# Half of the first attention's row maxima moved from the experts' stage in among its first exponentials, which go one head at a time

## The reference, cut to what matters

```python
# L0: group norm, 8 heads of 32 channels, full softmax attention, residual
weight = softmax(einsum('bct,bcs->bts', q * scale, k * scale))
a = einsum('bts,bcs->bct', weight, v)
x = xf + proj(a)
# L1: layer norm, causal attention over 8 heads, residual
t = t + attn(ln_t(t))
# experts: layer norm, top 2 of 32 experts of width 64, sigmoid gates, all computed, gated
h = relu(einsum('td,edh->teh', xt, keys))
t = t + einsum('teh,te,ehv->tv', h, w, values)
```

## Time and profile before

| | |
|---|---|
| median of 3 runs | 4272.27 us (4267.15 to 4276.54) |
| span of the profiled execution | 4288.4 us |
| PE busy | 3671.0 us (86%) |
| DVE busy | 2027.4 us (47%) |
| ACT busy | 1710.8 us (40%) |
| POOL busy | 771.3 us (18%) |
| DMA | 263.84 MB, mean 62 GB/s |
| maxima on DVE (line 1044) | 983.4 us in 1024 instructions |

### The profile page before, as it was taken

One profiled execution on the slowest core, in us unless ns is written; L12 is line 12 of the kernel. 1 busy time (PEld: TensorE's weight loads), 2 busy tenths in 40 slices (PEclk: granted clock), 3 DMA queues, 4 the chain that ended last, 5 costly groups with the idle time before them and its releaser, 6 DMA issues.

```text
span 4288.4 us, 55007 instructions
## 1 busy us (share of the span) xinstructions
PE 3671.0 (86%) x18386; PEld 2033.9 (47%) x18386; DVE 2027.4 (47%) x2857; ACT 1710.8 (40%) x2732; POOL 771.3 (18%) x1051
## 2 busy tenths in 40 slices
PE   5898789987898878988889888898889987999867
PEld 3344563445634456344653445534464344644445
DVE  6334572355723566245652446424563345733533
ACT  1354335442354423634236342453334533354422
POOL 0000251002600035000430005300052001610035
PEclk7798899988998889989899798997898978999879
DMA  3011340114402143021420224202341113411134
GB/s 89 1 40 30 91 115 24 40 30 107 116 7 55 29 113 102 16 51 41 114 79 16 55 55 110 65 19 51 71 113 46 31 39 80 119 31 40 30 82 117
DMA packets 229749, 263.84 MB, mean 62 GB/s; under 512 B 137424, under 2 KB 139472, under 8 KB 229328
## 3 DMA queue, kind: packets, MB, share of 16 engines
q1 hardware_dynamic: 73808, 124.88, 12.1%
q0 software_dynamic: 155648, 135.17, 11.9%
HBM read 145.80 MB, written 9.44 MB: 36 GB/s over the span
## 4 chain that ended last, share of the span: by engine, by line
PE 57%; DVE 13%; DMA 11%; issue 8%; ACT 6%; POOL 2%; SPq 2%; DVEq 0%; ACTq 0%; POOLq 0%
PE ps_acc L586 9%; PE ps_two L684 9%; PE ps_acc L595 9%; DVE tops L1044 7%; DMA probs<-gates_dram 7%; PE ps_two L653 7%; PE ps_one L530 4%; DMA expert_sb<-experts_dram 3%; PE ps_one L531 3%; PE ps_one L532 3%; PE ps_one L684 3%; POOL nat L488 2%; SPq L414 1%; PE ps_one L718 1%; PE ps_one L725 1%
## 5 line engine op out<-in xcount | busy, mean ns | idle before, releaser
L1044 DVE TENSOR_REDUCE tops<-ps_two 128x1 bf16<-128x1024 f32 (+7 forms) x1024 | 983.4, 988 | 547.6 <-PE ps_two L656 401.1
L653 PE MATMUL ps_two<-stacks 96*128 96x512 f32 (+2 forms) x1792 | 664.5, 469 | 267.6 <-DVE tops L1044 198.6
L852 ACT ACTIVATE probs<-ps_two 128x1024 f32<-128x1024 f32 (+1 forms) x704 | 666.4, 963 | 385.0 <-PE ps_two L684 301.3
L476 POOL DMA_DIRECT2D expert_sb<-experts_dram x256 | 143.2, 561 | 2743.0 <-DVE rsum L1051 2608.9
L653 PEld LDWEIGHTS ps_two<-stacks 96*128 96x128 f32 x1792 | 355.8, 221 | 468.1 <-DVE tops L1044 270.9
L684 PE MATMUL ps_two<-stacks 97*128 97x512 f32 (+3 forms) x1408 | 525.4, 455 | 40.0 <-ACT probs L852 24.1
L684 PEld LDWEIGHTS ps_two<-stacks 97*128 97x128 f32 x1408 | 233.9, 195 | 523.7 <-issue 431.4
L586 PE MATMUL ps_acc<-probs,v_sb 128*32 128x512 f32 (+3 forms) x3584 | 466.8, 595 | 15.6 <-DVE rsum L1051 5.8
L595 PE MATMUL ps_acc<-probs,ones 128*32 128x512 f32 (+3 forms) x3584 | 452.2, 578 | 0.0
L488 POOL TENSOR_TENSOR nat<-expert_sb,nat 128x256 fp32r<-128x256 f32 x512 | 379.8, 746 | 369.8 <-ACT nat L795 271.3
L795 ACT CAST nat<-expert_sb 128x256 fp32r<-128x256 f32 x256 | 103.1, 406 | 831.5 <-DVE probs L1133 591.6
(11 more groups left out here) (128 smaller groups left out, 4721.8 us busy)
## 6 DMA issues: line engine op xcount, KB each, us to landing
stacks<-nat SPq DMA_DIRECT2D x792, 128.0 KB, 2.5
expert_sb<-experts_dram POOLq DMA_DIRECT2D x256, 256.0 KB, 5.2
probs<-gates_dram POOLq DMA_DIRECT2D x256, 256.0 KB, 8.6
x_in<-x_in_dram SPq DMA_DIRECT2D x9, 1024.0 KB, 4.9
out_dram<-x_res SPq DMA_DIRECT2D x16, 512.0 KB, 4.9
probs<-mats_dram SPq DMA_DIRECT2D x1, 2048.0 KB, 9.3
gates_dram<-w_turn SPq DMA_DIRECT2D x64, 16.0 KB, 1.5
sel_w<-sel_dram SPq DMA_DIRECT2D x1, 32.0 KB, 8.4
```

Of the source, the lines that this page charges most:

```text
L653: mm = pe.matmul(acc[:, c0:c1], q_st[0:MID, g, j, P * i:P * i + P], k_st[0:MID, g, j, c0:c1], start=True, stop=not diag)
L852: done(act.activation(probs[:, n % 2, per * i:per * i + per, a:HALF], acc[:, :, a:HALF], ACT.Exp, scale=SCALE), s + (i,))
L1044: done(dve.reduce_max(tops[:, j, i:i + 1], acc[:, 0:cols(st, i)], AX_X), s)
```

## The change

The list for a batch no longer has all 64 maxima ahead of the mixes. Only those of the first half of the queries (hf 0, both groups: 32 maxima and 8 rows) stand there, spread among the ups in the body and by themselves in the head. Those of the second half are spread among the mixes of the first half: group 0's among the mixes 1 to 7 of group 0, and group 1's among the mixes, "div" and "fin" steps behind group 1's first mix. As they need the wide banks, all mixes of the first half but the very first become narrow. The other edits only let a mix find the mix before it by its key, as the two can differ in the flag.

```diff
     def batch(self, experts):
-        tops = rows_later(self.top(0, 0, 0) + self.top(0, 0, 1) + self.top(0, 1, 0) + self.top(0, 1, 1))
+        tops = rows_later(self.top(0, 0, 0) + self.top(0, 1, 0))
...
-        a, b, c, d = (self.mix(0, g, hf, True) for hf in (0, 1) for g in (0, 1))
-        steps += a[:1] + ([("down", 1)] if experts else []) + a[1:] + b[:1] + [("norm", 0, 0, 0), b[1], ("div", 0, 0, 0), b[2], ("fin", 0, 0, 0)] + b[3:]
+        a, b, c, d = (self.mix(0, g, hf, hf == 1) for hf in (0, 1) for g in (0, 1))
+        a[:1] = self.mix(0, 0, 0, True)[:1]
+        steps += a[:1] + ([("down", 1)] if experts else []) + spread(a[1:], rows_later(self.top(0, 0, 1)))
+        m = [b[1], ("div", 0, 0, 0), b[2], ("fin", 0, 0, 0)] + b[3:]
+        steps += b[:1] + [("norm", 0, 0, 0)] + spread(m, rows_later(self.top(0, 1, 1)))
...
+    def mix_at(sec, st, g, hf, k):
+
+        return next(m for m in sec.no["mix"] if m[1:5] == (st, g, hf, k))
...
-                                times_values(("mix", st, g, hf, k - 1, wide))
+                                times_values(mix_at(sec, st, g, hf, k - 1))
...
-                            sums(("mix", st, g, hf, k - 1, wide))
+                            sums(mix_at(sec, st, g, hf, k - 1))
```

More of the change, by code:

```diff
@@ L241, in last_tile @@
         return (PH * (hf + 1) if st else TT) - 1
+    def mix_at(sec, st, g, hf, k):
+        return next(m for m in sec.no["mix"] if m[1:5] == (st, g, hf, k))
     def last_mix(sec, s):
         _, st, g, hf = s
-        return next(m for m in sec.no["mix"] if m[1:5] == (st, g, hf, last_tile(st, hf)))
+        return mix_at(sec, st, g, hf, last_tile(st, hf))
     def half(hf):
```

## The result

The changed kernel takes 4436.76 us (median of 4 runs, 4426.32 to 4438.52) against 4269.71 for the one before: 3.9% slower, ratio 1.039 with a 95% interval of 1.037 to 1.041. Forecast were 4399 and +126.6 us; measured are +167. The time lies within the range.

The account below looks back on a forecast made before the run. The gates' DMA loop was taken to bound the experts' stage, PE the first exponentials. Seven bodies at +31.2 - 10.4 and the head at -19.0 gave +126.6 us, 4399 us from the 4272.27 median; range 4320 to 4470.

Parts of the forecast that it names:

- The experts' stage can give 14.4 us at most: Experts' stage, 151.6 us per body: cannot fall below the closing section's 137.22 us, however much is taken out.
- the 10.4 I took: Experts' stage: expected saving of 10.4 us per body, bounds 6 to 14.4.
- the 2.4 us for products that find DVE busy and the 1.6 for the tail: Experts' stage: deductions from 14.4 us for products behind reductions, and for the last R and first mix's scores.
- a loop through the gates' DMA: Experts' stage: waiting for gates sets 12.90 us per three ups, 4.30 each, 137 us for 32.
- PE's work of 17.0 us is added whole: First exponentials: PE is never idle there, so 32 moved maxima and 8 row steps add 17.0 us per batch.
- The stalls, 14.2 us: First exponentials: PE waits for DVE reductions through two wide banks, 14.2 us per batch, making 31.2 with the work.
- Narrow mixes at 0: First exponentials: making the mixes narrow costs nothing, bounds -1 to +1 us per batch.
- The clock: Mixes: rival in which five of fifteen run at the lower clock, 108 us on top, 4507 us; chance 8%.
- the 85 to 93 that the prediction gave as its sign: Last residual add to group 1's norm: 85 to 93 us instead of 58 would show the forecast right.
- The head, -19.0: Head, no experts: eight heads' maxima fewer save 50.2 us, the mixes add 31.2, so 19.0 us less.
- The faster rival: Mixes: maxima hide among the exponentials, only PE's work is added, 15 us less in all, 4257 us; chance 7%.
- The one by which the experts' stage gives nothing back: Experts' stage: the body's gates' loop is slow by itself, not by maxima; +199 us, 4471 us; chance 10%.

Follow-up runs that it names:

- the second profile: The kernel before, unchanged, profiled once more: 4264.11 us, span 4262.2 us.
- lifting the experts' alone: Changed kernel with the expert's load and ScalarE's casts of product and values moved earlier, gates still issued last: 4463.49 us.
- lifting both: Gates issued first, and expert's load and ScalarE's product and value casts earlier: 4340.11 us on the changed kernel, 4213.96 on the one before.
- the narrow form alone: Changed kernel with all 64 maxima back in the experts' stage, first exponentials still narrow: 4262.54 us, ratio 0.9986 to before.
- The head alone: Kernel before with the change made in batch 0 only, loop bodies as before: 4262.45 us, ratio 0.9968.
- the short reductions: Changed kernel with each moved maximum taken over 128 keys instead of 1024, so output differs: 4307.80 us, ratio 1.010 to before.
- the first sixteen maxima: Only a quarter of the 64 maxima moved, group 1's second half, spread over both groups' mixes: 4278.31 us, 4188.38 with both loops lifted.
- early gates: GpSimd issues the gates' load first in its up step: 4442.13 us on the changed kernel, 4269.97 us on the kernel before.

## Why the prediction was right, and where it was off

The sign, the mechanism and the range held. By its steps:

- *The experts' stage can give 14.4 us at most.* Right, and nearly reached: against the 10.4 I took, 13.8 (from the second profile) to 14.1 (from the first) came back. Of the 2.4 us for products that find DVE busy and the 1.6 for the tail only 0.3 to 0.6 were there. The reason given, a loop through the gates' DMA, was half of the truth: the arithmetic of 12.90 us for three ups fitted, and so did that of a second loop. Lifting the gates' alone moved nothing, lifting the experts' alone left the stage at 142, lifting both brought 127. The number held all the same, because the bound was read from the closing section's time (137 us), whatever sets it.
- *PE's work of 17.0 us is added whole.* Right: 18.5 us of busy PE left the experts' stage, and with reductions that take a quarter of the time the stretch was still 24.9 us longer. What arrived is more, 25.6 us of busy PE; the clock's lower level is in it.
- *The stalls, 14.2 us.* Right in size. The fourteen gaps of one body, each from its first T or R to the next scores, sum to 16.5 in group 0 and 16.7 in group 1 (forecast 15.6 each), so 33.2 against 31.2; most kinds were 0.1 to 0.2 us longer (TTT 2.63 against 2.43, TTTT 3.83 against 3.61), RTT and the last ones as forecast within 0.1.
- *Narrow mixes at 0.* Right in the time of the narrow form alone (0.9986); by the windows it is some 1.2 us a batch at the same clock, just over the bound of 1. In company it is worse: the wait of group 1's first mix, 0.86 us, comes right behind the wait of 1.98 for the last row, and the clock fell there. At the lower level values and sums took 1.94 us each.
- *The clock.* This is the term that was mis-sized. I had it as a rival with 8%, of five slow mixes, and left it out of the sum, though in the first profile of before all seven bodies stood at 0.91 to 0.94 in this stretch; in the second four are at 1.00 and 54.7 us. The changed kernel never is: 0.91 or 0.95 in all seven. Gaps of 33.2 leave 5.5 us of the 38.7 for the narrow start and the clock together; no run splits them. With them the stretch came to 94.4 us, above the 85 to 93 that the prediction gave as its sign.
- *The head, -19.0.* The head alone measured -14 (8 to 19). Its maxima end 50.8 us earlier (50.2 forecast), but from there to group 1's norm its mixes take 96 us instead of 58: they carry 38 us, not 31.

Against the second profile of before: 7 x (38.7 - 13.8) = 174, less 6 for the head's part and some 6 elsewhere, is the 162 us between the two spans (the head's part is its lead up to the first gated product of body 1, 509.11 against 515.35). Of the 36 us by which the forecast was short of that, some 52 are the mixes (7 x 7.5), 13 the head, -24 the experts' stage and -6 elsewhere. The stage hid a third of the other two's error; that much of the nearness is luck.

The faster rival is ruled out by the short reductions. The one by which the experts' stage gives nothing back is ruled out by the windows. What the Trainium skill's page "Perfetto Trace Analysis", section "Optimization Strategy", says of interleaving stages with different most-contended engines held here at best for the first sixteen maxima, which came out even (4278.31 us, ratio 1.0012; with both loops lifted they gained), and not for the next.

What stays open is why the clock falls at just these places. In all seven bodies it fell behind the waits of 3.33, 1.98 and 1.99 us; behind the 0.94 and 0.40 among four maxima (1242.49, 1243.62) it fell in three of seven, and behind the single waits of 0.85 to 1.01 of group 0 in none.

## What to carry to other kernels

Work that moves between stages is priced at the margin of each: what the stage that loses it can give back (here its time in a section that never had it, 137 us), and what the stage that gets it adds to its bound engine, stalls included. The price of each maximum is not the same: sixteen were even, thirty-two cost 3.9%, because the second sixteen gave 3.5 us back for 24.5. A loop whose arithmetic fits the period isn't thereby the only one; edit it, and if nothing moves, look for a second one of the same length, for lifted together they gave 1.3% to the kernel before and 2.2% to the changed one.

## What the runs showed of the hardware that was not expected

With early gates GpSimd's pairs of subtractions took 1.88 us where they had taken 1.57, and DVE's subtraction beside them 0.80 instead of 0.68: they run at the same time in that kernel. The timeline with early gates:

```profile
4334.45 1.88 POOL L495 TENSOR_TENSOR nat<-expert_sb,nat 128x256 fp32r<-128x256 f32 x2 [0.52 <-ACT nat L802]
...
4334.92 0.80 DVE L967 TENSOR_TENSOR nat<-probs,nat 128x512 fp32r<-128x512 f32 x1 [0.96 <-ACT nat L928]
```

The Trainium skill's page "Perfetto Trace Analysis", section "Optimizing Scalar/DVE Operations", says that GpSimd and DVE share a read port of SBUF; the trace agrees in that both were slower side by side, by 0.31 (for the pair) and 0.12 us. With both loops lifted DVE is at times held up for longer than GpSimd's subtraction takes: 64 of its 252 subtractions took over 1.2 us, as here, in the changed kernel with both, beside one of 0.75 on GpSimd.

```profile
1656.18 1.63 DVE L967 TENSOR_TENSOR nat<-probs,nat 128x512 fp32r<-128x512 f32 x1
...
1656.50 0.75 POOL L495 TENSOR_TENSOR nat<-expert_sb,nat 128x256 fp32r<-128x256 f32 x1
```

And two profiles of one and the same kernel differed by 26 us in span (4288.4 and 4262.2). In the first exponentials the difference was 16 us (405.79 and 389.76), and it goes with the granted clock: 54.7 us at 1.00, 56.2 at 0.97, 57.2 to 57.7 at 0.94, 58.6 at 0.91.
